# Attention heads: maxima 22 rows ahead instead of 32, split and normalised on GpSimd, both transposes taken by ScalarE, later loads in four portions

## The reference

```python
q = split_heads(embedding @ Wq + bq)      # HEADS = 16, HDIM = 8
k = split_heads(embedding @ Wk + bk)
v = split_heads(embedding @ Wv + bv)
scores = jnp.einsum('bhqd,bhkd->bhqk', q, k) * scale
attn = jax.nn.softmax(scores, axis=-1)
av = jnp.einsum('bhqk,bhkd->bhqd', attn, v)
out = av.transpose(0, 2, 1, 3).reshape(b, s, e) @ Wo + bo
```

## Time and profile before

| | |
|---|---|
| time, median of three runs | 2015.67 us (2013.53 to 2017.98) |
| the profiled execution's own time | 2017.86 us |
| its span, first to last instruction | 2015.8 us |
| PE, DVE, ACT, POOL busy, share of the span | 83%, 80%, 58%, 32% |
| granted TensorE clock, mean over the span | 0.911 |
| first crossed score | 65.27 us |
| first score | 109.67 us |
| last normalising of the heads stage ends | 782.82 us |

### The profile page before, as it was taken

One profiled execution on the slowest core, in us unless ns is written; L12 is line 12 of the kernel. 1 busy time (PEld: TensorE's weight loads), 2 busy tenths in 40 slices (PEclk: granted clock), 3 DMA queues, 4 the chain that ended last, 5 costly groups with the idle time before them and its releaser, 6 DMA issues. The chain is left out here.

```text
span 2015.8 us, 47315 instructions
## 1 busy us (share of the span) xinstructions
PE 1676.4 (83%) x15985; PEld 893.6 (44%) x15985; DVE 1607.9 (80%) x3367; ACT 1168.3 (58%) x2378; POOL 653.3 (32%) x354
## 2 busy tenths in 40 slices
PE   6689999999999997499999596999995843676777
PEld 3123322332323224266666363666663532575645
DVE  6689999998999973589999574898995877677556
ACT  5068877887888885188888422788884200332411
POOL 3020000000000002488788224777873333223101
PEclk9579999999999998699999898999998975887889
DMA  5710100000100001100000121000002220010022
GB/s 167 186 26 23 28 19 18 17 22 22 25 18 18 2 2 47 47 21 20 23 23 19 43 74 32 22 20 23 23 20 53 73 74 21 1 32 22 23 64 73
DMA packets 141050, 74.94 MB, mean 37 GB/s; under 512 B 50978, under 2 KB 135772, under 8 KB 140636
## 3 DMA queue, kind: packets, MB, share of 16 engines
q1 hardware_dynamic: 129008, 65.00, 11.7%
q10 hardware_dynamic: 11884, 7.84, 1.6%
HBM read 51.56 MB, written 20.98 MB: 36 GB/s over the span
## 5 line engine op out<-in xcount | busy, mean ns | idle before, releaser
L657 DVE TENSOR_REDUCE hd_top<-hd_pX 128x1 f32<-128x512 f32 x1024 | 620.5, 679 | 32.0 <-PE hd_pX L535 31.7
L640 ACT ACTIVATE hd_E<-hd_pS 128x1024 f32<-128x1024 f32 x512 | 524.2, 1024 | 199.9 <-PE hd_pS L550 183.0
L535 PE MATMUL hd_pX<-l_K,l_Q 48*128 48x512 bf16 x1024 | 354.7, 404 | 24.6 <-DMA l_Q<-q_parts 23.2
L567 PE MATMUL hd_pO<-hd_E,l_V 128*32 128x256 f32 x4096 | 331.0, 395 | 16.5 <-ACT hd_O L633 16.3
L550 PE MATMUL hd_pS<-l_Q,l_K 50*128 50x512 bf16 x1024 | 318.4, 388 | 11.1 <-issue 6.2
L1132 POOL TENSOR_TENSOR w_inv<-w_ss,w_mhalf 128x16 f32<-128x16 f32 x64 | 186.2, 2910 | 124.0 <-DVE w_ss L1161 124.0
L1080 ACT ACTIVATE w_pS<-w_pS,w_nb 128x128 f32<-128x128 f32 x512 | 175.6, 344 | 1.6
L519 POOL COPY l_V<-l_v_all 128x256 f32 x12 | 4.8, 400 | 495.0 <-PE hd_pO L567 495.0
L567 PEld LDWEIGHTS hd_pO<-hd_E,l_V 128*32 128x32 f32 x4096 | 82.1, 108 | 171.2 <-issue 108.2
L550 PEld LDWEIGHTS hd_pS<-l_Q,l_K 50*128 50x128 bf16 x1024 | 61.6, 94 | 209.0 <-issue 197.1
L1121 POOL TENSOR_TENSOR w_C<-w_C,w_N 128x1024 f32<-128x1024 f32 x64 | 150.8, 2356 | 0.0
(11 more groups left out here) (207 smaller groups left out, 3080.2 us busy)
## 6 DMA issues: line engine op xcount, KB each, us to landing
l_Q<-q_parts SPq DMA_DIRECT2D x192, 32.0 KB
l_K<-k_parts SPq DMA_DIRECT2D x180, 32.0 KB
m<-w_Y SPq DMA_DIRECT2D x64, 64.0 KB, 1.6
f_H<-m SPq DMA_DIRECT2D x32, 128.0 KB
f_X<-m SPq DMA_DIRECT2D x16, 256.0 KB, 3.1
q_parts<-pj_ptq SPq DMA_DIRECT2D x8, 384.0 KB, 2.5
k_parts<-pj_ptk SPq DMA_DIRECT2D x8, 384.0 KB, 2.5
pj_X<-in_L_attn_embedding_dram SPq DMA_DIRECT2D x8, 256.0 KB, 3.1
```

The source lines that it names most:

```text
L535: nc.tensor.matmul(pX[slot][:, :], Q[m.j][rows, m.z, b, t * P:(t + 1) * P], K[m.j][rows, b, k * 512:(k + 1) * 512], start=True, stop=True) ...
L567: last = nc.tensor.matmul(pO[VW * b:VW * b + VW, cols], V[n.j][:, b * NT + g, :], E[g % SLOTS][:, b, cols], start=(g == 0 and half == 0), ...
L640: nc.scalar.activation(E[g % SLOTS][:, 2 * k:2 * k + 2, :], pS[k][:, :, :], ACT.Exp).then_inc(exped[k], 1)
L657: nc.vector.tensor_reduce(top2[m.z][:, ROW_ORDER[q], k:k + 1], pX[slot][:, :], AX.X, ALU.max).then_inc(topped, 1)
```

## The change

- Crossed scores run 22 rows ahead of the scores, not 32. In unit `n`, steps 0 to 4 cross rows 6 to 15 of unit `n + 1`, and steps 5 to 7 rows 0 to 5 of unit `n + 2` (`in_stream`). The fold of `n + 1` comes at step 4, its turning at step 5, closing at step 2.
- GpSimd splits the maxima before they are turned (`part_neg`: three operations on 128 x 16), so that PE turns 32 columns; it also normalises (`norm`), with a power of -1 in place of the reciprocal, from a copy `OS` in SBUF.
- ACT copies both turned tiles out of their banks (`take_neg`, `take_out`), behind its exponentials of the same step.
- `Banks` tells PE what lay in a bank before: for a turned tile PE waits for ACT's copy.
- SP loads heads 0 and 1 at the start (K of both by ACT), and head h + 2 behind the stores of maxima of head h (`head`). Its loop runs over heads 4 to 11, other heads are written out.
- The later phases' loads are issued by SP in four portions, behind the second half's maxima of heads 0 to 3; GpSimd's multiplications and casts for them come in units 27, 28 and 29, and V's copies behind `norm` and `part_neg`.

```diff
+    AHEAD = 22
+    FOLD_AT = (2 * ROWS - AHEAD) // 2 - 1
+    TURN_AT = FOLD_AT + 1
+    CLOSE_AT = 2
...
+        def in_stream(g, after, after2):
+
+            row = AHEAD - ROWS + 2 * g
+            return (after, row) if row < ROWS else (after2, row - ROWS)
+
...
+                def load_both(h, j):
+                    load(sp, h, j, Q, q_parts, 0)
+                    load(sp, h, j, K, k_parts, 1)
+
+                def head(h, j):
+
+                    store_neg(1, h, j)
+                    if isinstance(h, int) and h < 4:
+                        kept.load(sp, a, h)
+                    if not (isinstance(h, int) and h + 1 >= H):
+                        store_neg(0, h + 1, (j + 1) % R)
+                    if not (isinstance(h, int) and h + 2 >= H):
+                        if not (isinstance(h, int) and h + 2 < R):
+                            sp.wait_ge(scored[1], 2 * NT * (h + 2 - R + 1))
+                        load_both(h + 2, (j + 2) % R)
+
+                for h in range(2):
                     load(sp, h, h, Q, q_parts, 0)
-                    load(sp, h, h, K, k_parts, 1)
                 store_neg(0, 0, 0)
-                with sp.Fori(1, H // R) as i:
+                for h in range(R):
+                    head(h, h)
+                with sp.Fori(1, H // R - 1) as i:
                     for j in range(R):
-                        h = R * i + j
-                        store_neg(1, h - R, j)
-                        store_neg(0, h - R + 1, (j + 1) % R)
-                        sp.wait_ge(scored[1], 2 * NT * (h - R + 1))
-                        load(sp, h, j, Q, q_parts, 0)
-                        load(sp, h, j, K, k_parts, 1)
+                        head(R * i + j, j)
                 for h in range(H - R, H):
-                    store_neg(1, h, h % R)
-                    if h + 1 < H:
-                        store_neg(0, h + 1, (h + 1) % R)
+                    head(h, h % R)
...
+                def part_neg(m):
+
+                    pool.wait_ge(folded[m.z], m.h + 1)
+                    pool.wait_ge(neg_turned[m.z], m.h)
+                    one = ones[:, :].broadcast_to([P, ROWS])
+                    nc.gpsimd.tensor_tensor(high[m.z][:, :], neg[m.z][:, :], one, ALU.mult).then_inc(neg_high, 1)
+                    pool.wait_ge(neg_high, m.n + 1)
+                    nc.gpsimd.tensor_tensor(neg2[m.z][:, 0, :], high[m.z][:, :], one, ALU.mult)
+                    nc.gpsimd.tensor_tensor(neg2[m.z][:, 1, :], neg[m.z][:, :], high[m.z][:, :], ALU.subtract).then_inc(neg_parted[m.z], 1)
+
+                def norm(n):
+                    pool.wait_ge(o_taken, n.n + 1)
+                    pool.wait_ge(normed, n.n)
+                    sums = OS[:, :].rearrange("p (t b c) -> p t b c", t=QT, b=B)
+                    power = minus[:, :].rearrange("p (t b) -> p t b", t=1).broadcast_to([P, QT, B])
+                    nc.gpsimd.tensor_tensor(inv[:, :, :], sums[:, :, :, HD], power, ALU.pow).then_inc(inverted, 1)
...
+                def unit(n, before, after, after2):
+                    if not n.is_first():
+                        norm(before)
+                    if after.exists():
+                        part_neg(after)
...
+                    if n.known == UNITS - 5:
+                        kept.prepare_tables(pool, 0)
+                    if n.known == UNITS - 4:
+                        kept.prepare_tables(pool, 1)
+                    if n.known == UNITS - 3:
+                        kept.prepare_casts(pool)
...
+                def bank(kind, tops):
+
+                    slot, held, back = banks.take(kind)
+                    if held == "neg":
+                        pe.wait_ge(neg_split[turned[0].z], turned[0].h + 1)
+                    elif held == "out":
+                        pe.wait_ge(o_taken, turned[1].n + 1)
+                    elif not isinstance(tops, int) or tops > back:
+                        pe.wait_ge(topped, tops - back)
+                    return pX[slot]
...
-                for m in (Unit(0, 0), Unit(0, 1)):
-                    for q in range(ROWS):
+                for m, rows in ((Unit(0, 0), ROWS), (Unit(0, 1), AHEAD - ROWS)):
+                    for q in range(rows):
...
-                kept.load(act, a)
+                kept.load_ident(act, a)
+                load(act, 1, 1, K, k_parts, 1)
...
+                def take_neg(m):
+                    act.wait_ge(neg_turned[m.z], m.h + 1)
+                    if m.known is None or m.known > 1:
+                        act.wait_ge(neg_stored[m.z], NEGS * m.h)
+                    slot, _, _ = banks.take("neg")
+                    nc.scalar.copy(negp[m.z][:, :], pX[slot][0:MAX_ROWS * ROWS, 0:P]).then_inc(neg_split[m.z], 1)
+
+                def take_out(n):
+                    act.wait_ge(o_turned, n.n + 1)
+                    act.wait_ge(normed, n.n)
+                    slot, _, _ = banks.take("out")
+                    nc.scalar.copy(OS[:, :], pX[slot][:, :]).then_inc(o_taken, 1)
...
+                        if g == TURN_AT and after.exists():
+                            take_neg(after)
+                        if g == CLOSE_AT and not n.is_first():
+                            take_out(before)
```

More of the change, by code:

```diff
@@ L513, in _ @@
                     nc.gpsimd.tensor_copy(V[h][:, :, 0:HD], v_all[:, :, h * HD:h * HD + HD]).then_inc(v_ready[h], 1)
[L514 to L519, removed]
+                nc.gpsimd.memset(ones[:, :], 1.0).then_inc(constants, 1)
@@ L521, in _ @@
+                part_neg(Unit(0, 0))
+                units(pool, unit)
+                norm(Unit(0, UNITS - 1))
             @block.tensor
@@ L554, in score_and_cross @@
                         if m.exists():
[L555 removed]
+                            cross(m, row + k, b)
                 def products(n, g, half):
@@ L633, in take_sums, with pass_tops @@
                     nc.scalar.copy(O[:, :], pO[:, :]).then_inc(o_ready, 1)
+                def take_neg(m):
[9 more added lines that the diff above has]
+                    nc.scalar.copy(OS[:, :], pX[slot][:, :]).then_inc(o_taken, 1)
+                def pass_tops(count):
+                    for _ in range(count):
+                        banks.take()
                 def unit(n, before, after, after2):
@@ L642, in unit @@
                                 take_sums(before)
-                units(act, unit)
+                        if in_stream(g, after, after2)[0].exists():
+                            pass_tops(TOPS // NT)
+                        if g == TURN_AT and after.exists():
+                            take_neg(after)
+                        if g == CLOSE_AT and not n.is_first():
+                            take_out(before)
+                pass_tops(TOPS)
+                take_neg(Unit(0, 0))
+                pass_tops(2 * (AHEAD - ROWS))
+                units(act, unit, banks)
                 take_sums(Unit(0, UNITS - 1))
+                take_out(Unit(0, UNITS - 1))
             @block.vector
@@ L654, in top @@
                     for k in range(2):
-                        slot, _ = banks.take()
+                        slot, _, _ = banks.take()
                         dve.wait_ge(crossed, TOPS * m.n + 2 * q + k + 1)
@@ L685, in _ @@
[L685 to L686 removed]
+                for m, rows in ((Unit(0, 0), ROWS), (Unit(0, 1), AHEAD - ROWS)):
+                    for q in range(rows):
                         top(m, q)
[L688 removed]
                     if m.n == 0:
[L690 removed]
+                        fold(m)
+                        banks.take("neg")
                 def unit(n, before, after, after2):
                     for g in range(NT):
[L694 to L702 removed]
+                        m, row = in_stream(g, after, after2)
+                        if m.exists():
+                            for q in range(row, row + 2):
+                                top(m, q)
+                        if g == FOLD_AT and after.exists():
+                            fold(after)
+                        if g == TURN_AT and after.exists():
+                            banks.take("neg")
+                        if g == CLOSE_AT and not n.is_first():
+                            banks.take("out")
```

198 lines of the change are left out of this document (88 added, 110 removed).

## The result

The changed kernel takes 2024.58 us (median of 6, 2022.87 to 2026.02), the kernel before 2016.05 (median of 6, 2012.44 to 2018.44): a ratio of 1.0044, interval 1.0031 to 1.0057. It is slower, by 0.44%. The profiled execution took 2022.87 us, its span is 2020.6.

A forecast was written before the change was run, and what follows sets the result against it. DVE was taken to set the mid-stage pace, PE close behind. Start -16.4, unit 0 -0.5, units +0.4, unit 30 +0.4, end +3.5 and clock +2.4 made -10.2 us on the median 2015.67: 2005.5 us, range 1981 to 2032.

The forecast's parts named there:

- The start: Start of the heads stage: first score at 93.3 instead of 109.67, 16.4 us earlier.
- The end: Last unit's normalising by ACT's copy and GpSimd's power and product, with nothing behind to hide it: +3.5 us.
- A wait for K once a head in SP's loop: PE waits for K's loads, issued behind the store of maxima: 1.7 us at every second unit in the loop.
- P, a unit without other waits: Length of an undisturbed unit in the heads stage: 19.3 + 0.75 = 20.0 us, bounds 19.3 and 20.6.
- The dry spells: DVE out of crossed scores at steps 1 and 2, from PE's lateness: 0.7 to 0.8 us a unit.
- The landing of K: Time from SP's last K issue until the data and its signal are there: 1.2 us.
- The late K: One slow K load group in each of the loop's two turns: +0.9 us each, 1.8 in all.
- The clock: PE's waits idle it 1.3 us, under the 1.9 for a clock fall; one late-K head counted at +2.4 us.
- Rival B: In the heads stage the clock falls at each wait and the kernel is slower: 2030 us, chance 0.2.
- the sum: All forecast gains and losses of the heads stage, fourteen heads loaded the new way: -10.2 us together.
- Rival A: In the heads stage loads come in time, so the waits and their costs go: -31.6, 1984 us, chance 0.2.
- Rival C: DVE stays short of scores and a unit stays at 20.6 us: 2014.5 us, no change, chance 0.15.

The follow-up runs named there:

- the last experiment: Loads first with the units' loop written out and the last unit's normalising back on DVE: 1981.2 us, ratio 0.9842 to the kernel before.
- loads first: The changed kernel with SP issuing the loads of head h + 2 before the store of unit 2h + 2's maxima: 2001.68 us, ratio 0.9917.
- SP written out: The changed kernel, order of loads kept, with only SP's loop over heads 4 to 11 written out: 2004.77 us, ratio 0.9932.
- the first experiment: The same run as loads first: the changed kernel with head h + 2's loads issued ahead of the store, 2001.68 us.
- three K early: The changed kernel with only three of the twelve K loads of head h + 2 issued before the store of maxima: 2001.83 us, ratio 0.993.

## Why the prediction was wrong

It said 2005.5 us and faster; it became 2024.58 and slower. The stage's end was to be at 782.82 - 10.2 = 772.6 and is at 790.87, 18.3 us later. By its steps:

- **The start** (93.3, -16.4 us): 92.61. Right, 0.7 better.
- **The end** (+3.5 us): copy at 786.82, end at 790.87, 4.05 us; DVE's way took 0.6. Right, and the last experiment takes it back.
- **A wait for K once a head in SP's loop** (shown by loads first and by SP written out): right in place and cause. Outside the loop five of the six expected waits of 0.6 us are not there and one is 0.41, for K is issued in 4.2 us, not 4.75, in four of these heads; with the longer P a pair of units is 40.7 us all the same (40.6 forecast): two errors that cancel, which is luck.
- **P, a unit without other waits, 20.0 us: the first term mis-sized.** It is 20.33. The dry spells are as forecast (0.18 + 0.22 + 0.32 = 0.72). But maxima in a row overlap: each takes 0.684 and starts 0.598 after the last, and wherever DVE runs dry that overlap of 0.086 is lost too. Four runs of maxima in a unit take 3.67 + 8.46 + 2.48 + 4.88 = 19.49 where 32 x 0.598 is 19.14.
- **The landing of K, 1.2 us after the last issue: the second.** It is 1.76: the data ended 0.9 after it, and 0.8 more passed before PE started, where I had given the signal 0.4 or less. The value that I set aside, my estimate of 1.8 from the fixed cost of about 2.0 us in the Trainium skill (DMA: Bandwidth & Descriptors, Anatomy of one DMA), agrees with the 1.76 of this queue: the row that I preferred showed the end of the data, and PE did not start with that. With a gap of 0.28 to 0.63 us ahead of Q and Q's issue of up to 10.3, from turn to crossed score it takes 19.90 to 20.54 us instead of 19.2. The late K of 0.9 us twice did not come. Two units with one wait take 42.6 us in the mean, without the clock, where 41.9 were forecast: 5.4 us over eight heads.
- **The clock: the step that failed.** "My waits idle PE for 1.3 us, under 1.9", and one fall of 2.4 us. The waits idled it for 1.84 to 2.48, 2.12 in the mean, where Rival B was to decide from 1.9, and five falls cost 12.9 us, 10.5 more than in the sum. The bound itself was no bound: 1.43 us sufficed once, 2.38 did not once. I had it from one pause, and from the moment of the fall within it; four of the five falls here come 0.3 to 1.2 us after PE has resumed. The Trainium skill's warning (TensorE: Matmul & The Clock Gate, HAM oscillation), that a DMA wait in each tile can bring the clock down tile after tile, agrees with five of eight.

5.4 + 10.5 are 15.9 of the 18.3; P in the other units adds 0.7 and the end 0.6, the start takes off 0.7, and 1.8 are not assigned; about 1 of them is that two of the eighth units (the second and the 26th) are longer by 0.5 than the rest, which the sum did not have. **Rival B** happened in the main: its condition (the chain 0.6 longer) came as 0.56 of landing and the slow issues, its price per fall (2.35) was 2.6 in the mean; it had 2030 for seven falls and a longer wait in all fourteen heads. **Rival A**, loads in time, is the first experiment: the sum has 10.2 + 1.8 + 2.4 + 17.2 = 31.6 us for it against the kernel before, and 17 were measured: P is 0.33 longer in thirty units (9.9 us), and the first score of that run comes 1.9 later than forecast. **Rival C** is out: P is not 20.6, though nearer to it than to 19.3.

The deeper error is in the odds. A chain of issues that ends 1.7 us after its need, on a sum of 20, left no room: 0.6 us more on it, and the clock's 12.9 us came on top of the waits' 15.4. I had the clause and gave it 0.2.

## What to carry to other kernels

When a load's issue is moved behind another instruction of an in-order queue, count from the event that releases that instruction: every issue behind it, then the time to the reader's start (1.8 us here, 0.8 of it after the data's end), against the time of the need. SP's issue of one and the same twelve loads varied here from 8.5 to 10.5 us; so if the sum comes out within about 2 us of the need on either side, treat the wait as there and add the clock's price. And look for the free exchange first: here the same calls in another order turned a loss of 0.4% into a gain of 0.8%. And where two engines have the same floor, neither's floor is the pace: PE work added was paid at three quarters, DVE work removed at less than half.

## What the runs showed of the hardware that was not expected

- In most cases the granted clock fell to 0.50 after PE had resumed: at 362.1 after a wait that ended at 361.08, in three K early 2 us after it. Waits of 1.43, 1.87, 1.95, 2.26, 2.30 and 2.48 us of idle had a fall behind them, others of 1.84, 1.89 and 2.38 had none. What decides between them no run here shows.
- The stay at the lower level behind such a wait lasted 3.4 to 10.2 us (488.0 to 491.4; 631.8 to 642.0) with PE at work all along, and cost 1.1 to 4.0 us.
- SP issues the same twelve loads of Q in 8.5 to 9.6 us written out and in 9.65 to 10.3 in a loop with computed addresses, twelve of K mostly in 4.2 (up to 4.9) and in 4.75.
- The units' loop stops the engines for about 3 us at each turn (3.00 and 2.86 us of PE idle in the changed kernel), and with the low clock behind it a turn cost 5.2 and 6.2 us in loads first (26.01 and 27.02 against 20.85 without the loop), 3.8 at the first turn of the changed kernel (24.63).
- DVE's maxima from PSUM, in a row, take 0.684 us each and start 0.598 apart; each time that DVE runs dry costs the overlap of 0.086 beside the idle time, 0.34 in a unit with four runs of maxima.
